# A GNN and expert layer on one core: one ring of slots freed tile by tile, two scatters moved into the experts, selections over three pairs of PSUM banks

## The reference

```python
grouped = x.reshape(B, S // t, t, D)                       # x is layer-normed
cont_logits = einsum('bgtd,des->bgtes', grouped, controller) + tie
cont_perm = (cont_logits == max(cont_logits, axis=-3)).astype(x.dtype)
intermediate = einsum('bgtd,desf->bgtesf', grouped, f1)
inner = relu(einsum('bgtesf,bgtes->bgesf', intermediate, cont_perm))
inter2 = einsum('bgesf,esfd->bgesd', inner, f2)
result = einsum('bgesd,bgtes->bgtd', inter2, cont_perm)     # added to x
```

## Time and profile before

| | us |
|---|---|
| median of 3 runs | 768.1 |
| lowest, highest | 761.76, 772.48 |
| the profiled execution | 766.25 |
| its span | 764.3 |
| TensorE busy in the span | 712.9 (93%) |
| VectorE busy | 596.2 (78%) |
| ScalarE busy | 546.3 (71%) |
| mean granted TensorE clock | 0.986 of full speed |

### The profile page before, as it was taken

The page is one execution under the profiler, slowest core; times in us unless marked ns, Lnnn a source line. Parts: engine busy times, 40 slices in busy tenths (PEclk is TensorE's granted clock), DMA queues, the critical chain, the costliest instruction groups (busy, mean ns, idle before and its releaser), DMA issues.

```text
span 764.3 us, 22954 instructions
## 1 busy us (share of the span) xinstructions
PE 712.9 (93%) x7420; PEld 570.7 (75%) x7420; DVE 596.2 (78%) x2418; ACT 546.3 (71%) x1606; POOL 180.7 (24%) x375
## 2 busy tenths in 40 slices
PE   7899999999999999999999999988879879887987
PEld 7778888888888888888888887766645655654775
DVE  6789898898898898988988988876656646655654
ACT  4889988989898999889998988845344344353332
POOL 2130230321312302303213122747225225200000
PEclk9999999999999999999999999999999999988999
DMA  7877886787687777867876777560699798699902
GB/s 179 202 172 164 178 194 147 178 195 161 163 192 168 184 168 168 194 146 178 195 164 162 168 166 160 132 205 31 270 323 291 291 315 277 252 323 314 330 30 83
DMA packets 110742, 149.24 MB, mean 195 GB/s; under 512 B 14784, under 2 KB 75712, under 8 KB 110432
## 3 DMA queue, kind: packets, MB, share of 16 engines
q1 hardware_dynamic: 107904, 146.26, 71.0%
q10 hardware_dynamic: 2592, 1.71, 1.0%
q0 software_dynamic: 192, 0.52, 0.2%
HBM read 39.39 MB, written 33.55 MB: 95 GB/s over the span
## 4 chain that ended last, share of the span: by engine, by line
PE 78%; DMA 10%; DVE 4%; ACT 4%; issue 2%; SPq 1%; ACTq 0%; DVEq 0%
PE bank L651 15%; PE bank L603 14%; PE bank L638 8%; PE bank L664 8%; PE bank L675 8%; PE bank L625 7%; DMA stage<-scratch 5%; DMA scratch<-stage 4%; PE bank L834 3%; PE bank L792 3%; PE bank L849 3%; PE bank L876 2%; ACT stage L1091 2%; PE bank L596 2%; PE bank L696 1%
## 5 line engine op out<-in xcount | busy, mean ns | idle before, releaser
L997 ACT ACTIVATE Ps<-Ps,nmax 128x256 f32<-128x256 f32 x512 | 254.6, 501 | 19.8 <-DVE nmax L1217 19.8
L1217 DVE CUSTOM_DVE_ANT_0 Ps<-bank,masks 128x256 f32<-128x256 f32 x512 | 192.7, 419 | 27.6 <-issue 27.6
L651 PE MATMUL bank<-ident,Ps 128*128 128x128 f32 x1024 | 134.7, 274 | 2.6 <-ACT Ps L997 1.9
L651 PEld LDWEIGHTS bank<-ident,Ps 128*128 128x128 f32 x1024 | 114.8, 141 | 12.0 <-issue 3.3
L603 PE MATMUL bank<-hT,WT 128*128 128x256 f32 x512 | 121.0, 380 | 0.4 <-ACT hT L954 0.4
L603 PEld LDWEIGHTS bank<-hT,WT 128*128 128x128 f32 x512 | 92.4, 190 | 10.7 <-ACT Vs L970 0.8
L528 POOL TENSOR_SCALAR h<-X,mv,roots 128x256 f32<-128x256 f32 x64 | 79.3, 1250 | 85.3 <-PE bank L792 83.1
L997 ACT ACTIVATION_READ_ACCUMULATOR Ps<-Ps,nmax 128x1 f32 x512 | 97.5, 190 | 0.0
L638 PE MATMUL bank<-stack 128*128 128x256 f32 x512 | 91.5, 311 | 0.5 <-DMA stack<-parts 0.4
L1228 DVE COPY PTs<-bank 128x512 f32<-128x512 f32 x128 | 86.3, 674 | 0.2
L638 PEld LDWEIGHTS bank<-stack 128*128 128x128 f32 x512 | 71.6, 189 | 17.5 <-issue 13.1
(11 more groups left out here) (107 smaller groups left out, 1059.8 us busy)
## 6 DMA issues: line engine op xcount, KB each, us to landing
stack<-parts SPq DMA_DIRECT2D x506, 128.0 KB, 2.5
scratch<-stage SPq DMA_DIRECT2D x48, 512.0 KB, 5.0
stage<-scratch SPq DMA_DIRECT2D x96, 256.0 KB, 4.5
X<-in_x SPq DMA_DIRECT2D x32, 256.0 KB, 3.0
out<-X SPq DMA_DIRECT2D x32, 256.0 KB, 3.8
rbc<-turned SPq DMA_DIRECT2D x126, 64.0 KB, 2.1
f1s<-in_L_ffn_f SPq DMA_DIRECT2D x1, 2048.0 KB, 8.3
f2s<-in_L_ffn_f SPq DMA_DIRECT2D x1, 2048.0 KB, 14.2
```

Of the source, the lines that this page charges most:

```text
L651: last = nc.tensor.transpose(PTb[h % 2][:, k * N + t * P:k * N + t * P + P], Ps[:, pr % 2, t, h % 2, k * P:k * P + P], ident[:, :])
L997: last = nc.scalar.activation(Ps[:, pr % 2, t, h, :], Ps[:, pr % 2, t, h, :], ACT.Exp, bias=nmax[:, pr % 2, t, h:h + 1], scale=-1.0, accum ...
L1217: last = nc.vector.tensor_tensor_reduce(out=Ps[:, pr % 2, t, h, :], in0=s_bank(n)[:, h * N:h * N + N], in1=masks[:, t, :], scale=1.0, scal ...
```

## The change

Five things, all in the expert layer:

- Selections write three pairs of banks in turn, (4, 5), (6, 7), (0, 1), starting anew with each unit (`pair_of`). Banks 0 and 1 are also those of `unit_transpose`; waits for h2T and for the copies keep the two apart.
- Contractions write banks 4 to 7 in each step, and wait for both engines' copies of the step before. The waits for fin_done and for the one-hots at w = 0 go.
- All uses of the slots, 16 quads and 16 tiles of each chunk, are numbered on in one ring (`quad_turn`, `tile_turn`), slot = turn % 5. sc_ready counts tiles instead of pairs, and a gather waits for the one tile that had its slot.
- EARLY is 4 instead of 3.
- Scatters of chunk c - 1 stand two in each of units 1, 2 and 3, after select(2) and after select(3). The last two (tiles 12 to 15, LATE) stand in the experts of chunk c, ahead of contract(0) and contract(1); VectorE's finish of each ahead of the copies of that step. The group maximum comes ahead of the first finish, the one-hot behind the second.

```diff
+        def pair_of(t, hf):
+            return (4, 6, 0)[(2 * t + hf) % 3]
...
-            return ((), (0, 1), (2, 3, 4), (5, 6, 7))[u]
+            return ((), (0, 1), (2, 3), (4, 5))[u]
+        LATE = (6, 7)
...
-        def tile_slot(tile):
-            return (tile + 1) % SLOTS
+        def quad_turn(c, q):
+            return c * (QUADS + CT) + q
+        def tile_turn(c, tile):
+            return c * (QUADS + CT) + QUADS + tile
+        def turns_of(turn, tiles):
+            return sum(1 for t in range(turn % SLOTS, turn + 1, SLOTS) if (t % (QUADS + CT) >= QUADS) == tiles)
+        def landed(c, q):
+            return turns_of(quad_turn(c, q), False) * 16
+        def tiles_read(c, tile):
+            return c * CT + tile + 1
...
                 if tile >= SLOTS and half == 0:
-                    sp.wait_ge(sc_ready, c * (CT // 2) + (tile - SLOTS) // 2 + 1)
+                    sp.wait_ge(sc_ready, tiles_read(c, tile - SLOTS))
...
-            EARLY = 3
+            EARLY = 4
...
                 for hf in range(2):
-                    if tile > 0:
+                    if t == 0 and n > 0:
                         pe.wait_ge((sel_dve, sel_act)[hf], tile)
+                    elif (t, hf) == (1, 0) and n + AHEAD < CHUNKS * UNITS:
+                        pe.wait_ge(h2T_saved, n + AHEAD + 1)
+                    elif (t, hf) == (1, 0):
+                        pe.wait_ge(sel_act, tile - 2)
+                    elif t > 0:
+                        pe.wait_ge((sel_act, sel_dve)[hf], tile - 1 + hf)
...
-                for hf in range(2):
-                    if 2 * w + hf >= PAIRS_OF_BANKS:
-                        pe.wait_ge((st_dve, st_act)[hf], 2 * (n - 1 + hf))
+                if n > 0:
+                    pe.wait_ge(st_act, 2 * n)
+                    pe.wait_ge(st_dve, 2 * n)
...
                 if ahead:
+                    if n > 0:
+                        pe.wait_ge(sel_act, n * UT - 1)
                     unit_transpose(n + AHEAD)
...
-                if pairs:
-                    scatter(c - 1, pairs[0])
                 select(n, 1)
                 if ahead:
                     logits(n + AHEAD)
                 select(n, 2)
                 if pairs:
+                    scatter(c - 1, pairs[0])
+                select(n, 3)
+                if pairs:
                     scatter(c - 1, pairs[1])
-                select(n, 3)
-                if len(pairs) > 2:
-                    scatter(c - 1, pairs[2])
...
                     if w + 1 < TWOS:
                         expand(c, w + 1)
+                    if c > 0 and w < len(LATE):
+                        scatter(c - 1, LATE[w])
                     contract(c, w)
...
-                        if landed(c, q) > 16:
-                            act.wait_ge(moved[q % SLOTS], landed(c, q) - 16)
+                        if q >= SLOTS:
+                            act.wait_ge(moved[quad_slot(c, q)], landed(c, q - SLOTS))
...
-                if pairs:
-                    finish(c - 1, pairs[0])
                 save_selected(c, u, 1)
...
                 save_selected(c, u, 2)
                 late_root_steps(c, u, 2)
+                if ahead:
+                    group_maximum()
+                if pairs:
+                    finish(c - 1, pairs[0])
+                save_selected(c, u, 3)
+                late_root_steps(c, u, 3)
                 if pairs:
                     finish(c - 1, pairs[1])
                 if ahead:
-                    group_maximum()
-                save_selected(c, u, 3)
-                late_root_steps(c, u, 3)
-                if ahead:
                     one_hot(n + AHEAD)
-                if len(pairs) > 2:
-                    finish(c - 1, pairs[2])
```

More of the change, by code:

```diff
@@ L329, in chosen, with products @@
             return permT[region(tile // UT)][:, (tile % UT * 4 + j) * 32:(tile % UT * 4 + j) * 32 + 32]
[L331 to L339, removed]
+        def products(c, q, hf):
+            b = 4 + 2 * hf
+            return stage[:, quad_slot(c, q), 2 * hf:2 * hf + 2, :], banks[:, b:b + 2, q % 2 * D:q % 2 * D + D]
         def stack_rows(par, j, r):
@@ L416, in move @@
                 sp.wait_ge(st_act, n + 1)
-                sp.dma_start(by_group(c, q), stage[:, q % SLOTS, :, :].rearrange("p j d -> p (j d)"))\
-                    .then_inc(moved[q % SLOTS], 16)
+                sp.dma_start(by_group(c, q), stage[:, quad_slot(c, q), :, :].rearrange("p j d -> p (j d)"))\
+                    .then_inc(moved[quad_slot(c, q)], 16)
             def gather(c, tile, half):
                 if tile >= SLOTS and half == 0:
-                    sp.wait_ge(sc_ready, c * (CT // 2) + (tile - SLOTS) // 2 + 1)
-                slot = tile_slot(tile)
+                    sp.wait_ge(sc_ready, tiles_read(c, tile - SLOTS))
+                slot = tile_slot(c, tile)
                 sp.dma_start(XR[half::2, slot, :, :], by_expert(c, tile, 1, half)).then_inc(gathered[slot], 16)
             def written(c, q):
-                sp.wait_ge(moved[q % SLOTS], landed(c, q))
+                sp.wait_ge(moved[quad_slot(c, q)], landed(c, q))
             def store(c, s):
@@ L827, in contract @@
                                 r = slice(32 * j, 32 * j + 32)
-                                last = nc.tensor.matmul(bank[first_bank(w, j // 2) + j % 2][:, i * D + k * P:i * D + k * P + P],
+                                last = nc.tensor.matmul(bank[4 + j][:, i * D + k * P:i * D + k * P + P],
                                                         f2s[r, q, k * P:k * P + P], inner[r, 2 * (w % RELUS) + i, :],
@@ L833, in contract @@
                             r = slice(32 * j, 32 * j + 32)
-                            last = nc.tensor.matmul(bank[first_bank(w, j // 2) + j % 2][:, i * D:i * D + D],
+                            last = nc.tensor.matmul(bank[4 + j][:, i * D:i * D + D],
                                                     inner[r, 2 * (w % RELUS) + i, :], f2s[r, q, :],
@@ L873, in scatter @@
                     tile = 2 * s + tt
-                    pe.wait_ge(gathered[tile_slot(tile)], arrived(c, tile))
+                    pe.wait_ge(gathered[tile_slot(c, tile)], arrived(c, tile))
                     for j in range(4):
                         last = nc.tensor.matmul(bank[3][32 * j:32 * j + 32, tt * D:tt * D + D],
-                                                chosen(c * CT + tile, j), XR[:, tile_slot(tile), j, :],
+                                                chosen(c * CT + tile, j), XR[:, tile_slot(c, tile), j, :],
                                                 start=True, stop=True)
-                last.then_inc(sc_ready, 1)
+                    last.then_inc(sc_ready, 1)
             def unit(c, u):
@@ L1466, in experts @@
                 for w in range(TWOS):
+                    if c > 0 and w < len(LATE):
+                        finish(c - 1, LATE[w])
                     dve.wait_ge(f2_ready, c * TWOS + w + 1)
```

52 lines of the change are left out of this document (22 added, 30 removed).

## The result

| | before | changed |
|---|---|---|
| median of 20 runs, us | 764.09 | 759.8 |
| lowest, highest | 761.69, 772.48 | 757.18, 763.67 |
| ratio, 95% interval | | 0.9918 (0.9897 to 0.9938) |
| span of the profiled execution | 764.3 | 757.3 |
| its mean granted clock | 0.986 | 0.993 |

What follows compares the result with a forecast made beforehand. Neither TensorE nor the DMA engines fill a round alone; the chain ending last in each stage bounds it. Eight stages summed to 208.0 us against 224.7, 16.7 less, giving 749.5, stated as 751 for small waits; range 743 to 762.

Steps and rivals of the forecast that it cites:

- a round of 53.0 us: Chunks 1 and 2: units 30.0 us plus experts 23.0, against units of 36.1 and 39.05 and experts of 19.95 and 21.8.
- the moves swallow the longer expert steps: Experts with moves: the moves need 23.6 us in any case, so they absorb most of the loss of longer steps.
- the sum for the last chunk: Last chunk: units 27.3 us against 36.1, experts 24.6 against 21.4, contract(1) starting about 27.5 us after the last move lands.
- every tile is there before its scatter: Gathers: tile t+5, asked for when tile t was read, lands some 5 us later, before its scatter; tile 3 0.2 late.
- the half select: Units: the second half of a select takes 0.34 us, so 0.33 of 0.77 us idle is won; unit 6.15 after 6.58.
- the account of the half clock: Half-clock stretches outside the first units, costing some 7 to 8 us, vanish with the waits for transfers.
- the rival of the bounding transfers: Every chunk: transfers keep their lengths, a round is 54.5 us, the last chunk 2 us longer; 756 us in all; 17%.
- each 0.8 us at the 330 GB/s: Last chunk: 28 half tiles still to come, 0.8 us each after a latency of some 3, done 25.4 us after the last move.
- scatters wait 27.3 us for gathered tiles: Reading of the earlier profile: what the gather stage loses in three chunks; a few us in all expected after the change.
- the step of 2.64 us: Experts: contract waits for all copies of the step before, VectorE's too, so a step takes 2.64 us instead of 2.42.
- the rival of a longer contract chain: Experts: VectorE does copies and inner in one row, 28 steps x 0.41 = 11.5 us more; 762 us, no measurable change; 10%.
- The slow rival: Experts: TensorE's share falls from 0.85 to 0.79, the clock to 1.2 GHz; 46 us more, 797 us; 5%.

Runs made afterwards that it cites:

- sel_only: The kernel before with only the selections over three pairs of banks; slots, scatters and contractions as before: ratio 1.003 (0.9987 to 1.0073).
- light gathers: Changed kernel, each gather bringing half its rows (128 KB instead of 256), result incomplete: ratio 0.9804; the kernel before with the same: 0.9851.
- two_pairs: The kernel before with only contractions on two pairs of banks, waiting for both engines' copies of the step before: ratio 1.000 (0.997 to 1.0031).
- after_fill1: Changed kernel plus idle identity multiplications: one ahead of contracts, four ahead of the turn back and the first unit's last select: 757.32 us, ratio 0.9892.
- best: Changed kernel, contractions over three pairs from step 2; idle multiplications: one ahead of contracts, four ahead of turn back and first unit's last select: 754.05 us.
- late_shift: Changed kernel, but in the last chunk scatters 6 and 7 stand ahead of contract(2) and contract(3): 760.08 us, ratio 0.9927.

## Why the prediction was off

The time, 759.8, lies within the range of 743 to 762, but the gain was a third of that forecast. The main mechanism named did come: the late scatters uncouple the experts from the last gather, TensorE's order gives a round of 53.0 us (without waits for gathers), and the moves swallow the longer expert steps. What failed above all is the sum for the last chunk, 51.9 us where 56.5 were measured, with its claim that every tile is there before its scatter; besides it the half select and the account of the half clock.

1. *"Unit without scatters: 6.58 - 0.43 = 6.15."* Measured 6.49. The step took a half select for half of the time of a whole one (0.34 us). Alone it needs 0.64, as the x8 row shows. sel_only confirms that the selections are worth nothing that can be measured. The first chunk's units came out at 28.2 us after 28.7 forecast, but by luck: some 0.6 of the 1.8 us are the selections and 1.2 the clock, which the sum had left at the 0.94 of before. Where scatters stand in the unit, the hole is filled by them: such a unit takes 7.9 us from one transpose group to the next (564.50 to 572.40) after the 7.8 forecast.

2. *"followed through all sixteen, each is there before its scatter."* In the rounds several tiles are late by some tenths, and the rounds are 1.7 and 2.0 us longer than with light gathers. At 54.7 and 55.0 us they took what the rival of the bounding transfers gave them, 54.5. In the last chunk the tiles are late by more: "each 0.8 us at the 330 GB/s" was the rate of the best stretch. The last row of units moved 297 GB/s at a share of 0.90.

3. *"Units 6.1 + 21.2 = 27.3 against 36.1"*, and experts of 24.6. Units and experts of the last chunk take 56.5 us, not 51.9, which is nearly half of what is missing. These rows of the changed kernel hold it:

```profile
683.92 0.66 PE L718 MATMUL bank<-ident,permT 128*128 128x128 f32 x4 [0.91 <-DVE permT L1311]
...
696.21 0.64 PE L892 MATMUL bank<-stage,permT 128*32 128x256 f32 x8 [1.38 <-DMA stage<-scratch]
...
700.68 0.64 PE L892 MATMUL bank<-stage,permT 128*32 128x256 f32 x8 [1.66 <-DMA stage<-scratch]
...
720.24 2.09 PE L843 MATMUL bank<-h2T,f2s 32*128 32x128 f32 x32 [1.49 <-DVE XS L1488]
```

In the third unit the one-hot transposes come sooner, for no transposes of h2 stand ahead of them, and wait 0.91 us for VectorE's one-hot: the sum has no term for this. Two scatters, of tiles 11 and 13, wait 1.38 and 1.66 us for a gather; by the sum every tile was there. And the last contract takes 2.09 us, where the others of its stage take 1.17: the clock has fallen. Together these are 4.9 us, about the 4.6 that the last chunk is longer than the sum.

4. *"In this sum all stretches of half clock but that of the first units are gone"*, 7 to 8 us. By the line of 0.57 us per 0.001 the profiled execution at 0.986 had lost 8.0 us to it, the mean run of before (0.9876) 7.1, and the mean run of the changed kernel (0.9923) still loses 4.4. So by this estimate 2.7 us came of it, not 7 to 8: the half clock went from the units, and a part of it came back in the last experts (0.93) and the turn back (0.95). *"and those waits are what the change takes away"* was the reason given, and it does not hold by itself: with light gathers, without any such wait, the last units have 0.89. What makes the clock fall there stays open. The other 3.1 us of the difference between the spans, 762.5 to 759.4 at 0.990, are work and waits. The base was a little high besides: the three runs shown had a median of 768.1, where those beside the other kernels have 764 to 766.

5. Ahead of the change, 1.3 us: the first select starts at 508.0 instead of 506.7. The change doesn't touch it; it varies between 506.2 and 508.1 over the profiles here.

In numbers, for the spans: forecast -16.7, measured -7.0; the difference of 9.7 is 1.1 in the units and experts of the first two chunks, 0.6 in chunk 2's units, 1.4 in its experts, 4.6 in the last chunk, 1.3 in the stretch ahead and 0.7 in the turn back. The clock of point 4 is no further term: what of it falls into this pair of executions is in these rows.

Two readings were wrong as well. "scatters wait 27.3 us for gathered tiles" counts weight loads and matmuls of the same scatters; the matmuls lost 10.7. And the clock fell in one of the four expert stages of the earlier trace rows, not in a third of them.

The parts that held: the step of 2.64 us to the hundredth, so that the rival of a longer contract chain fell; that the loss of the steps disappears in the moves (two_pairs); a round of 30.0 + 23.0, measured 30.6 + 22.4 with light gathers; that no wait of 2 us is left in chunks 1 and 2, with a clock of 1.00 in all four windows. The slow rival did not come: with TensorE busy for 0.79 of the first experts the clock stayed at 1.00 there. The rule of the Trainium skill on cycling through PSUM banks (TensorE: Matmul & The Clock Gate, A second HAM failure mode: psum-queue depth-cycling) is not borne out by the expert stages of chunks 0 to 2 here. The falls that are left came in the last experts and in the turn back; whether it had a part in them is not shown. after_fill1 and best, with those gaps filled, have mean clocks of 0.997 and 0.998.

What stays open: whether late_shift is worth the microsecond that the lines show, what the stores of the output cost the last gathers, and what part of best's gain over the changed kernel is the clock's and what part the steps'. after_fill1, which fills alike but keeps the steps of 2.64, stands 2.5 us below the changed kernel and best 3.3 below that, from four and six runs.

## What to carry to other kernels

When a stage starts only after the last transfer of the one before, let the work that needs this transfer slide into the next stage: here taking back two scatters placed in the next stage's first two steps cost all of the gain, while finer slots, an earlier gather and more banks for the selections were worth nothing that could be measured. Before summing stretches at half clock into a gain, look at the clock of many runs: a part of such stretches moves to other places. Count a wait once, on the engine that does the work, when two rows show it. And measure a piece of work by itself before taking it for half of the whole.

## What the runs showed of the hardware

Two halves of a select, of 32-row matmuls on different row groups (x8 records each), go through together: 16 records in 0.67 us, 8 alone in 0.64, and three halves in a row, x24, in 1.16 as the profile models it.

One identity multiplication in fp32 shows as two records, and in a row of three each takes 0.29 us (six records in 0.86 from start to start).

Mean granted clock and span of the same kernel fall about a line: 0.57 us for 0.001. As 0.001 of 764 us is 1.5 us at 1.2 GHz, one microsecond at the lower level goes with 0.37 us of span, less than half of it. This is an estimate from the runs of one kernel. after_fill1 fits it: 0.0047 more of mean clock, 2.5 us less. That it is less than half may come of copies and transfers that go on meanwhile; no run separates this.
